# Attention stage of a macaron block: fp32 products of x, two terms joined on the vector engine, one diagonal instead of two

## The reference

```
x = x + 0.5 * ffn(layernorm(x));  x = x + attn(layernorm(x));  x = x + 0.5 * ffn(layernorm(x))

attn:  delta, _, Cs, residual = split(x @ W_proj.T, 4)
       delta = softplus(delta @ W_delta.T + b_delta)
       dA = exp(delta * A1) * B1          # per position and feature
       dB = cumsum(delta * B1, axis=1)    # along the sequence
       uC = sum(x * Cs, axis=1); Csum = sum(Cs, axis=1)   # one number per batch and feature
       y = dA * uC + dB * Csum + residual * D
```

## Time and profile before

| | us |
|---|---|
| median of 3 runs | 1657.67 |
| profiled execution, its own time | 1659.85 |
| its span, first to last instruction | 1658.0 |
| TensorE busy in the span | 1384.7 |
| VectorE busy | 1190.8 |
| ScalarE busy | 1167.4 |
| GpSimd busy | 776.3 |

### The profile page before, as it was taken

How to read it: one execution, slowest core, us unless ns; L and a number is a source line. 1 busy time by engine, 2 the same in 40 slices (tenths; PEclk the granted TensorE clock), 3 DMA queues, 4 the chain that set the end, 5 groups by cost and what they waited for, 6 DMA issues and landing times. The chain is left out here.

```text
span 1658.0 us, 32704 instructions
## 1 busy us (share of the span) xinstructions
PE 1384.7 (84%) x10686; PEld 1297.6 (78%) x10686; DVE 1190.8 (72%) x3211; ACT 1167.4 (70%) x2458; POOL 776.3 (47%) x989
## 2 busy tenths in 40 slices
PE   4345531799999999779999999998747999999997
PEld 3223320699999999779999999998636999999997
DVE  5366644577788787567799888889655777777875
ACT  7568851577777777468888888887545777777774
POOL 0046566143443434334447778777452434434343
PEclk8555555799999999989999999999867999999999
DMA  9977844566666766340222223311115444444541
GB/s 366 372 235 250 267 151 144 176 207 226 219 220 204 237 220 196 144 143 14 78 78 82 88 79 93 94 56 48 38 43 151 123 123 135 138 140 123 157 139 36
DMA packets 196888, 250.10 MB, mean 151 GB/s; under 512 B 24650, under 2 KB 182008, under 8 KB 192624
## 3 DMA queue, kind: packets, MB, share of 16 engines
q1 hardware_dynamic: 169072, 204.23, 38.3%
q0 software_dynamic: 27648, 43.78, 7.5%
HBM read 128.05 MB, written 152.17 MB: 169 GB/s over the span
## 5 line engine op out<-in xcount | busy, mean ns | idle before, releaser
L978 PE MATMUL ps<-xs,ws 128*128 128x320 f32 x3072 | 466.3, 311 | 3.7 <-DVE hf L932 3.7
L978 PEld LDWEIGHTS ps<-xs,ws 128*128 128x128 f32 x3072 | 456.0, 190 | 4.8 <-issue 4.8
L347 POOL DMA_INDIRECT slots<-xn,r x256 | 261.6, 1022 | 239.1 <-issue 167.9
L805 POOL DMA_INDIRECT x_rows<-ys,oidx x160 | 155.9, 975 | 251.9 <-DVE ys L917 174.2
L805 POOL DMA_INDIRECT out<-ys,oidx x160 | 156.0, 975 | 248.7 <-DVE ys L917 170.7
L978 PE MATMUL ps<-ws,hs 128*128 128x256 f32 x1920 | 261.9, 288 | 11.0 <-DVE ys L917 7.5
L978 PEld LDWEIGHTS ps<-ws,hs 128*128 128x128 f32 x1920 | 238.7, 190 | 24.4 <-issue 22.3
L932 DVE TENSOR_TENSOR hf<-ps,sg 128x320 f32<-128x320 f32 x256 | 125.8, 492 | 144.5 <-issue 101.8
L415 PE MATMUL ps<-cf,xn 128*128 128x128 f32 x512 | 110.7, 355 | 109.2 <-ACT xn L369 95.4
L826 ACT CAST xs<-ps 128x512 fp32r<-128x512 f32 (+1 forms) x192 | 98.5, 514 | 130.0 <-PE ps L971 130.0
L415 PEld LDWEIGHTS ps<-cf,xn 128*128 128x128 f32 x512 | 73.9, 178 | 144.8 <-ACT xn L369 118.2
(11 more groups left out here) (119 smaller groups left out, 2428.3 us busy)
## 6 DMA issues: line engine op xcount, KB each, us to landing
slots<-zero SPq DMA_DIRECT2D x32, 1300.0 KB, 18.7
xg<-slots SPq DMA_DIRECT2D x62, 650.0 KB
x<-in_x SPq DMA_DIRECT2D x32, 512.0 KB, 10.8
x_rows<-x SPq DMA_DIRECT2D x32, 512.0 KB
wraw<-in_w_gate SPq DMA_DIRECT2D x64, 256.0 KB
wraw<-in_w_up SPq DMA_DIRECT2D x64, 256.0 KB
wraw<-in_w_down SPq DMA_DIRECT2D x64, 256.0 KB
x<-x_rows SPq DMA_DIRECT2D x32, 512.0 KB, 4.8
```

Of the source, the lines that this page charges most:

```text
L347: nc.gpsimd.indirect_dma_start(out=self.slots, out_offset=bass.IndirectOffsetOnAxis(ap=self.slot[:, t % self.xr, k:k + 1], axis=0), in_=se ...
L805: nc.gpsimd.indirect_dma_start(out=rows, out_offset=bass.IndirectOffsetOnAxis(ap=OIDX[:, e % YR, k:k + 1], axis=0), in_=YS[:, e % YR, k, : ...
L978: ins = pe.matmul(dst, left(a, k), right(b, k), start=(n == 0), stop=(n == len(terms) - 1))
```

## The change

- x is kept once, as turned, in fp32 (XS, written by ScalarE's copy). x_lo is gone. The weights WA are kept in fp32, unsplit.
- delta and residual use plain fp32 products: 4 of 256 columns for delta, 2 of 256 columns per tile for the residual.
- The size |u|, at least 1e-37, goes into the exponent: once per batch ScalarE computes log|u| + A1*b (size_bias), and d_a uses it as bias, so that YT holds |u|*exp(...).
- VectorE gets a new step mix, after scan: YT = CC * (c * sign u) + YT. It waits for scan and for d_a.
- One diagonal of the signs of u is left in place of two diagonals; the residual's matmuls wait for mix. a_factors computes size, sign and c*sign u.
- scan waits for an earlier mix instead of an earlier residual, and turn waits for ScalarE's copy instead of x_lo.
- In route(), the split of the weights goes.

```diff
-                            dve.tensor_copy(WT[:], ps[:, 7, :].rearrange("p (a b) -> p a b", a=2)).then_inc(s_prepd, 1)
-                            dve.tensor_scalar(WIN[:, 4:6, :], WIN[:, 4:6, :], DV[:, 0:1], None,
+                            dve.tensor_copy(WA[:, 0:2, :], ps[:, 7, :].rearrange("p (a b) -> p a b", a=2)).then_inc(s_prepd, 1)
+                            dve.tensor_scalar(WA[:, 2:4, :], WIN[:, 4:6, :], DV[:, 0:1], None,
                                               ALU.mult).then_inc(s_prepd, 1)
-                            dve.wait_ge(s_prepd, 2)
-                            dve.tensor_copy(WA[:, 0:2, :], WT[:])
-                            dve.tensor_copy(WA[:, 4:6, :], WIN[:, 4:6, :]).then_inc(s_prepd, 1)
...
+                    def size_bias(a):
+                        act.wait_ge(sized.sem, sized.at(a + 1))
+                        apart(act)
+                        act.activation(LB[:, a % 2, 0, :], UV[:, a % 2, 4, :], ACT.Ln).then_inc(size_links.sem, 1)
+                        act.wait_ge(size_links.sem, size_links.next())
+                        for h in range(HC):
+                            ins = act.activation(LB[:, a % 2, 1, h:h + 1], LB[:, a % 2, 0, h:h + 1], ACT.Identity,
+                                                 bias=ABD[:, h:h + 1])
+                        ins.then_inc(biased.sem, 1)
+
                     def d_a(n):
+                        a = n // NC
+                        if n % NC == 0:
+                            act.wait_ge(biased.sem, biased.at(a + 1))
...
-                                                 bias=ABD[:, h:h + 1], scale=A1[:, h:h + 1])
+                                                 bias=LB[:, a % 2, 1, h:h + 1], scale=A1[:, h:h + 1])
...
+                        for a in batches(S, 2):
+                            size_bias(a)
                         for n in at(S, PLUS):
                             d_a(n)
...
-                        for n in range(2):
-                            for h in range(HC):
-                                ins = dve.tensor_scalar(DIAG[:, a % 2, n, h, :], IDENT, uv[:, n, h:h + 1], None, ALU.mult)
+                        dve.scalar_tensor_tensor(uv[:, 2, :], uv[:, 0, :], -1.0, uv[:, 0, :], ALU.mult, ALU.max)
+                        dve.tensor_scalar(uv[:, 5, :], uv[:, 0, :], 0.0, 2.0, ALU.is_ge, ALU.mult).then_inc(f_links.sem, 1)
+                        dve.wait_ge(f_links.sem, f_links.next())
+                        dve.tensor_scalar(uv[:, 4, :], uv[:, 2, :], TINY, None, ALU.max).then_inc(sized.sem, 1)
+                        dve.tensor_scalar(uv[:, 6, :], uv[:, 5, :], -1.0, None, ALU.add).then_inc(f_links.sem, 1)
+                        dve.wait_ge(f_links.sem, f_links.next())
+                        dve.tensor_tensor(uv[:, 3, :], uv[:, 1, :], uv[:, 6, :], ALU.mult).then_inc(f_links.sem, 1)
+                        for h in range(HC):
+                            ins = dve.tensor_scalar(DIAG[:, a % 2, h, :], IDENT, uv[:, 6, h:h + 1], None, ALU.mult)
...
-                        dve.wait_ge(residual_done.sem, residual_done.at(n - 1))
+                        if n >= 2:
+                            dve.wait_ge(mixed.sem, mixed.at(n - 1))
...
+                    def mix(n):
+                        dve.wait_ge(scanned.sem, scanned.at(n + 1))
+                        dve.wait_ge(da_done.sem, da_done.at(n + 1))
+                        apart(dve)
+                        for h in range(HC):
+                            ins = dve.scalar_tensor_tensor(YT[:, n % 2, h, :], CC[:, n % 2, h, :],
+                                                           UV[:, n // NC % 2, 3, h:h + 1], YT[:, n % 2, h, :],
+                                                           ALU.mult, ALU.add)
+                        ins.then_inc(mixed.sem, 1)
...
-                        for n in at(S, DELTA):
-                            x_lo(n)
...
                         for n in at(S, PLUS):
                             scan(n)
+                        for n in at(S, PLUS):
+                            mix(n)
...
-                    terms = [(a, b, k) for k in range(HC) for a, b in ((0, 0), (0, 1), (1, 0))]
...
-                            for i, (a, b, k) in enumerate(terms):
+                            for k in range(HC):
                                 ins = pe.matmul(ps[:, BZ[n % 2], h * CT:(h + 1) * CT],
...
-                        pe.wait_ge(da_done.sem, da_done.at(n + 1))
-                        pe.wait_ge(scanned.sem, scanned.at(n + 1))
+                        pe.wait_ge(mixed.sem, mixed.at(n + 1))
                         pe.wait_ge(x_added.sem, x_added.at(n))
                         for j in range(CH):
...
+                            for k in range(HC):
+                                pe.matmul(ps[:, BY, j * H:(j + 1) * H], XS[:, n % 3, k, j * P:(j + 1) * P],
+                                          WA[:, 2 + k, :], start=(k == 0), stop=False, skip_group_check=True)
+                            for h in range(HC):
+                                ins = pe.matmul(ps[:, BY, j * H + h * P:j * H + (h + 1) * P],
+                                                YT[:, n % 2, h, j * P:(j + 1) * P], DIAG[:, t % 2, h, :],
+                                                start=False, stop=(h == HC - 1), skip_group_check=True)
```

More of the change, by code:

```diff
@@ L30 @@
 EPS = 1e-5
+TINY = 1e-37
 SL = CAP // 2
@@ L1044, in attention @@
                 b_turned = count("b_turned")
-                x_hi_done = count("b_hi")
-                x_lo_done = count("b_lo", 1)
+                x_kept = count("b_x_turned")
                 z_done = count("b_z")
@@ L1052, in attention @@
                 diag = count("a_diagonals")
+                sized = count("a_size")
+                biased = count("a_bias")
+                mixed = count("b_mixed")
                 residual_done = count("b_residual", 3)
+                size_links = Links(sem("a_size_log"))
                 x_added = count("b_x", 1)
@@ L1157, in x_hi @@
                         act.wait_ge(residual_done.sem, residual_done.at(n - 2))
-                        act.copy(XS[:, n % 3, 0].rearrange("p a b -> p (a b)"), ps[:, BX, :]).then_inc(x_hi_done.sem, 1)
+                        act.copy(XS[:, n % 3].rearrange("p a b -> p (a b)"), ps[:, BX, :]).then_inc(x_kept.sem, 1)
                     def softplus(n):
@@ L1206, in _ @@
                 def _(dve):
-                    for c in (sums_read, x_lo_done, softplus_done, scanned, x_added):
+                    for c in (sums_read, softplus_done, scanned, x_added):
                         c.grant(dve)
@@ L1252, in a_factors @@
                         dve.wait_ge(sums_read.sem, sums_read.at(a + 1))
-                        for n in range(2):
-                            for h in range(HC):
-                                ins = dve.tensor_scalar(DIAG[:, a % 2, n, h, :], IDENT, uv[:, n, h:h + 1], None, ALU.mult)
-                        ins.then_inc(diag.sem, 1)
-                    def x_lo(n):
-                        dve.wait_ge(x_hi_done.sem, x_hi_done.at(n + 1))
-                        dve.tensor_tensor(XS[:, n % 3, 1].rearrange("p a b -> p (a b)"), ps[:, BX, :],
-                                          XS[:, n % 3, 0].bitcast(F32).rearrange("p a b -> p (a b)"),
-                                          ALU.subtract).then_inc(x_lo_done.sem, 1)
+                        dve.scalar_tensor_tensor(uv[:, 2, :], uv[:, 0, :], -1.0, uv[:, 0, :], ALU.mult, ALU.max)
[7 more added lines that the diff above has]
+                            ins = dve.tensor_scalar(DIAG[:, a % 2, h, :], IDENT, uv[:, 6, h:h + 1], None, ALU.mult)
+                        ins.then_inc(diag.sem, 1)
+                        dve.wait_ge(f_links.sem, f_links.next())
                     def softplus(n):
@@ L1366, in turn @@
                         pe.wait_ge(normed.sem, normed.at(n + 1))
[L1367 removed]
+                        if n >= 1:
+                            pe.wait_ge(x_kept.sem, x_kept.at(n))
                         for h in range(HC):
@@ L1389, in residual @@
                             pe.wait_ge(diag.sem, diag.at(t + 1))
-                        pe.wait_ge(da_done.sem, da_done.at(n + 1))
-                        pe.wait_ge(scanned.sem, scanned.at(n + 1))
+                        pe.wait_ge(mixed.sem, mixed.at(n + 1))
                         pe.wait_ge(x_added.sem, x_added.at(n))
                         for j in range(CH):
-                            for i, (a, b, k) in enumerate(terms):
-                                pe.matmul(ps[:, BY, j * H:(j + 1) * H], XS[:, n % 3, a, k, j * P:(j + 1) * P],
-                                          WA[:, 4 + 2 * b + k, :], start=(i == 0), stop=False, skip_group_check=True)
-                            for i, src in enumerate((YT, CC)):
-                                for h in range(HC):
-                                    ins = pe.matmul(ps[:, BY, j * H + h * P:j * H + (h + 1) * P],
```

(5 more changed lines are left out.)

25 lines of the change are left out of this document (10 added, 15 removed).

## The result

The changed kernel takes 1668.58 us (median of 5 runs, 1666.09 to 1676.20) against 1657.67 for the kernel before beside it (5 runs, 1651.04 to 1665.96). The ratio is 1.0073, interval 1.0037 to 1.0109: **slower by 0.7%**, some 11 us, where 14 less were forecast; the time lies above the whole range. The profiled execution is the longest of the five, 1676.20, with a span of 1674.4. Part of its excess is scatter of what runs ahead of the attention block, which the change barely touches: the attention block begins (ScalarE's table load) at 711.9 there and at 703.1 in a second profile of the same kernel; in both profiles of the kernel before it begins at 705.9. I therefore compare lengths inside the attention block, and whole kernels by ratios taken on one chip.

What follows compares the result with a forecast made beforehand. TensorE was taken to bound the attention block, VectorE after the change. Gains of 6.3 (first steps), 5.2 (four batches), 3.3 (fifth) and -0.8 (end) total 14.0: median 1657.67 to about 1643.7, range 1628 to 1659.

Steps and rivals of the forecast that it cites:

- TensorE, -0.55 a step: Attention block, residual and delta: TensorE's products and diagonals fall from 4.87 to 4.29, taken as 0.55 less a step.
- VectorE does not hold it back: Rival for the attention steps: mix overlaps better or TensorE's lead absorbs uneven steps; 29 gained, 1629; chance 0.25.
- The bound changes hands: Attention batches: VectorE at 56.9 per eight steps overtakes TensorE at 54.7, leaving about 2.2 of TensorE's 4.4.
- Who waits for mix is the next residual: VectorE's queue in each attention step: the next residual waits for mix, with 3.9 of room, mix taking 1.0.
- 3.9 of room: One attention step: scan ended at 890.33, the residual needing it started at 894.22; mix takes 1.0 of that.
- VectorE stood only for some tenths: Walk through one attention batch: VectorE's standing taken as 0.3 to 1.5 per batch, middle 0.9, giving 57.8.
- my slower rival: Attention steps: VectorE stands at mix for d_a, kept behind the scan by ScalarE's order; 1680 or 1660; chance 0.07.
- decides from 2.2 a batch: Slower rival's condition: VectorE's standing at mix decides from 59.1 - 56.9 = 2.2 per batch, 0.28 a step.
- covered: size_bias on ScalarE, once a batch: under 1 us, hidden by ScalarE's room; uncovered it would cost 0.6 to 2.
- First 13 steps, -6.3: 736.39 to 827.60, before the expert choice: TensorE stays the bound, 13 x 0.55 = 7.2, taken as 6.3 gained.
- Weights' split at nothing: First block: removing the weights' split, about 2 us of VectorE, gains 0, at most 2, since VectorE then waits 3.12.
- the stall near the end in place: TensorE's slow matmuls from 1187.71 to 1196, some 8 us lost, were assumed to stay; chance of vanishing 0.2.

Runs made afterwards that it cites:

- e5: Kernel before with fp32 products of x, no rounded halves or x_lo, two diagonals, no mix, no size in the exponent: ratio 1.0222 to the kernel before.
- e2: Changed kernel with x_new ahead of mix on VectorE, nothing else: 1619.0 against 1622.16 for the kernel before, ratio 0.9974.
- e6: Changed kernel with the rounded halves and x_lo kept, so mix alone is tried: ratio 1.0154 to the kernel before.
- r3: Changed kernel with x_new ahead of mix on VectorE, on the same chip as r2: ratio 1.0033 to the kernel before.
- r2: Changed kernel, unchanged, run again on one chip with the kernel before: ratio 1.0072 to the kernel before.
- e9: Changed kernel with x_new ahead of mix and a_factors one step earlier: 1656.52 against 1659.89 for the kernel before, ratio 0.9976.
- e11: Changed kernel with x_new ahead of mix and without the size in the exponent (no size_bias): ratio 1.0020 to the kernel before.
- e4: Changed kernel without the size in the exponent (size_bias and d_a's wait for it gone): ratio 1.0047 to the kernel before.
- e10: Changed kernel with a_factors one step earlier, x_new still behind mix: ratio 1.0042 to the kernel before.
- e1: Changed kernel without mix, the residual waiting for scan and d_a: 1611.88 against 1622.16 for the kernel before, ratio 0.9934.
- e7: Changed kernel with x_new and the tail's statistics ahead of mix on VectorE: ratio 1.0117 to the kernel before.
- r5: Changed kernel without the size in the exponent, repeating e4 on another chip: ratio 1.0051 to the kernel before.

## Why the prediction was wrong

- **TensorE, -0.55 a step: mis-sized, -0.25.** The direct reason is in the rows after: an fp32 product with fresh weights costs 0.43 in the residual, as the Gram row said, but 0.47 in delta (1.87 / 4), 0.15 in all; the turn went from 0.35 to 0.43; the kept diagonals cost 0.45 twice, 0.90 against 0.85. Together 0.28 of the missing 0.30. I had called the turn unchanged and given it no row. Over 53 steps this costs 16 of the 29 that the rival "VectorE does not hold it back" would have had, and it is why, as long as TensorE sets the steps, no placement can gain more than about 13 in them (53 times 0.25).

 The Trainium skill, "FP8 and Floating Point Precision", section "TensorE Precision Notes", has true fp32 at four passes through the array. At an estimated 0.107 a pass of 256 columns that is 0.43: the residual's 0.43 agrees, delta's 0.47 lies above it. For a rounded pass the prediction had 0.13 from the rows and an estimated 0.107 by the page, and e5 comes out between: eight exchanges lost 0.56, where the rows gave 0.24 and the estimate from the page 0.85.

- **"The bound changes hands": wrong as it was meant.** VectorE's sum of work was about right: from R(24) to R(48), 180.5 less 12.3 of waits, it is occupied 7.01 a step where I had 7.11 (the median mix takes 0.48 per instruction, 0.43 by the earlier trace rows). But that is 56.1 a batch, and TensorE's own length turned out 57.08 and not 54.7. TensorE still has the longer list, and with x_new first (e2) it sets batches of 57.1 to 57.3; VectorE holds it back by its order, once a batch. Only where x_lo is kept besides mix (e6) does VectorE's work itself set the pace, 64.0 a batch.

- **"Who waits for mix is the next residual": the step that failed.** There are two chains to the next residual. One is mix of its own pair, to which I gave 3.9 of room. The other is x_new of the pair before, which frees the PSUM bank that the residual writes, and in the new order x_new is queued behind mix. Once a batch this is the last wait:

```profile
913.43 0.21 ACT L1173 ACTIVATE a<-a 128x2 f32<-128x2 f32 x1 [2.52 <-DVE a L1268]
...
913.88 1.26 DVE L1291 TENSOR_TENSOR_SCAN a<-vec,a 128x256 f32<-128x256 f32 x2
...
915.41 1.15 DVE L1300 SCALAR_TENSOR_TENSOR a<-a 128x256 f32<-128x256 f32 x2 [0.26 <-ACT a L1187]
...
916.48 0.68 DVE L1308 TENSOR_TENSOR x<-x,ps 128x512 f32<-128x512 f32 x1
...
917.30 0.89 PE L1417 MATMUL ps<-wa,a 128*128 128x256 f32 x3 [1.87 <-DVE x L1308]
```

 TensorE had finished that pair's residual at about 910.6; its result lay ready for 5.9 us while VectorE did softplus, a_factors, scan and mix. My text even said that x_new could start a little before the scan's end, and used it for 0.1 of price instead of asking who waits for x_new. r3 against r2 shows the step: the same work with x_new first is 0.4% better on one chip. My "3.9 of room" for mix was the room of one step only; in e9 and e11, where x_new is out of the way, it is mix of its own pair that the residual waits for once a batch, 1.0 to 1.5.

- **"VectorE stood only for some tenths" (0.3 to 1.5 a batch): 2.5 to 3.** In light steps mix waits for d_a, which ScalarE does behind the norms:

```profile
888.98 1.08 ACT L1187 ACTIVATE a<-a,vec 128x256 f32<-128x256 f32 x2
...
890.19 0.88 DVE L1300 SCALAR_TENSOR_TENSOR a<-a 128x256 f32<-128x256 f32 x2 [1.82 <-ACT a L1187]
```

 The standing falls into steps in which VectorE is early, and makes it late for the heavy ones. This is the mechanism of my slower rival, of chance 0.07, at a fraction of its price; its condition "decides from 2.2 a batch" was met. (Of its two distances in the earlier trace rows the first is 0.40 by the rows, not 0.36; it changes nothing.) Its missing half was the order on VectorE and on ScalarE. I had walked one batch with durations, but without a list of who waits for what behind each.

- **size_bias "covered": right in the batches** (e4, 59.4 with it gone), **wrong at the end.** I had written that with the cover gone it costs 0.6 to 2 and that d_a stands behind it. What stands behind it also are the tail's copies, for which TensorE's counts wait; it stood 3.58. Together with x_new it makes nearly all of the +6.9 of four steps: with both gone (e11) 0.6 is left. From R(56) to the end of the last residual I had 0.8 lost; it was 4.9 (88.9 against 93.8 on one chip). The worst term of my sum was still that of the batches: 8.5 gained forecast, 2.9 lost measured.

- **First 13 steps, -6.3: measured about 0** (+3.0 at the first pair, -2.6 behind it). The first residual waits for all of a_factors, scan and mix; e9 and e10 take a_factors away from there and get the 3.5 us back.

- **Weights' split at nothing, the stall near the end in place: right.** Without the split VectorE waits 3.11 for x at the place where it waited 3.12. R(64) to R(65), the step with the stall, is 18.8 before and 19.3 after; 20.5 and 19.5 in the pair on one chip. On the chip of e1 to e4 it is 9 to 10 with any version, so it belongs to neither kernel.

The sum by measured terms, on one chip: twelve steps -2.6, batches +2.9 (-10.1 from TensorE's five times 2.02, +13.0 from the waits, 10.4 of it in the five steps with the wait for x_new), first pair +3.0, last batch +6.9, rest -1.4: +8.8, against +12 by the ratio. The other 3 us lie outside the block or in scatter; I did not find them, and the two profiles do not show them: there the rest of the kernel is 4.3 shorter after the change.

## What to carry to other kernels

When a change puts work into an engine's fixed order, list what is queued behind it and ask for each of these who waits for it; here most of the loss came from x_new behind mix and from a copy behind size_bias. The new work itself is not free either: with x_new first, the kernel with mix is 0.4% above the one without it (e2 against e1). A stage that releases another engine goes ahead of a stage that is only needed later, and once-a-batch work belongs in a step where nobody waits. Where the gain hangs on one instruction's cost, take it from a row with the same neighbours, the operations around it included, since they pay too.

## What was not expected of the hardware

**Half clock after a wait.** TensorE's granted clock falls to the lower of its two levels (1.2 of 2.4 GHz) after some waits and stays there for some us, so that the wait is paid about twice: in the changed kernel after waits of 3.06 and 4.16, in e7 after 2.01 to 2.14 in four batches of five, which are 61.2 to 61.4 against 59.0 for the one without, and in e10 after 2.05 to 2.06 in four batches, 61.6 to 61.7. In the profile after, one batch has it at 977.0 behind a wait of 2.01, for 3.5 us:

```profile
977.00:980.50 3.50, 3.50 (x11) 2.96 (x12) 3.33 (x10) 3.50 (x9) 3.01 (x4) 0.51 0.66 191
```

The wait of 1.21 (e9) and one of 1.87 (after) were followed by full speed; in r5 two short ones close together, 1.29 and 0.89, were not. The length of the wait alone does not decide: one of 2.02 in r2 kept full speed (at 969.1), one of 1.87 in r5 did not (at 914.8, a batch of 63.1). What does decide stays open here. It makes lengths jump: 59.5 and 61.4 are two batches of the same work, without and with such a spell.

**GpSimd and VectorE lengthen each other.** The same order gave batches of 57.2 in e2 and 59.5 in e11. Lines of r3 in a batch of 57, and of e11 in the like place:

```profile
951.94 0.66 DVE L485 SCALAR_TENSOR_TENSOR r<-r,cf 128x512 f32<-128x512 f32 x1
...
955.58 1.40 DVE L1291 TENSOR_TENSOR_SCAN a<-vec,a 128x256 f32<-128x256 f32 x2
```

```profile
953.33 1.54 POOL L338 TENSOR_SCALAR x<-x,r 128x256 f32<-128x256 f32 x2
953.39 1.06 DVE L485 SCALAR_TENSOR_TENSOR r<-r,cf 128x512 f32<-128x512 f32 x1
...
957.28 1.84 DVE L1286 TENSOR_TENSOR_SCAN a<-vec,a 128x256 f32<-128x256 f32 x2
957.37 1.96 POOL L338 TENSOR_SCALAR x<-x,r 128x256 f32<-128x256 f32 x2
```

Where GpSimd's pass over x (L338) overlaps them, VectorE's operations take 1.06 instead of 0.66 and 1.84 instead of 1.40, and in e11 the residual at 969.9 then waits 1.29 for mix. In the changed kernel mix itself ranges from 0.47 to 0.88 per instruction. The Trainium skill, "SBUF — State Buffer", section "SBUF: two separate sides", describes a port pair that a VectorE operation with two SBUF inputs and a GpSimd operation take from each other for a whole instruction; the rows agree in kind, 0.4 more on VectorE's side, and on GpSimd's 1.54 and 1.96 for a pair of instructions that takes 1.10 at its shortest (r3 at 968.4). mix is such an operation and x_lo, which read PSUM, was not, so the change may have made VectorE more exposed to it; that this is where e11's two us come from is argued from these rows, and no run has tried it.
